# A decoder's two attentions: the low parts of the values set beside the high ones, two matmul passes in place of three, and the two halves of the output bank added afterwards

## The reference, cut to what matters

```
a0: y = layernorm(x); q, k, v = y@Wq.T, y@Wk.T, y@Wv.T   (16 heads of 32)
    x = x + softmax(causal(q k.T / sqrt(32))) v @ Wo.T
a1: y = rms_norm(layernorm(x)) * w; q, k, v = y@w_in.T   (32 query heads, 8 key groups, of 64)
    q, k = rope(q), rope(k)
    x = x + softmax(causal(q k.T / 8)) v @ w_out.T
```

## Time and profile before

| | us |
|---|---|
| runs shown (3) | 1926.97, 1926.93, 1922.9 (median 1926.93) |
| profiled execution | 1936.33 |
| its span, first to last instruction | 1934.9 |
| TensorE busy | 1813.6 (94%) |
| VectorE, ScalarE, GpSimd busy | 1116.9, 804.9, 1009.1 |
| mean granted TensorE clock | 0.980 of 2.4 GHz |

### The profile page before, as it was taken

One profiled execution on the slowest core, in us unless ns is written; L12 is line 12 of the kernel. 1 busy time (PEld: TensorE's weight loads), 2 busy tenths in 40 slices (PEclk: granted clock), 3 DMA queues, 4 the chain that ended last, 5 costly groups with the idle time before them and its releaser, 6 DMA issues.

```text
span 1934.9 us, 30810 instructions
## 1 busy us (share of the span) xinstructions
PE 1813.6 (94%) x10167; PEld 1568.5 (81%) x10167; DVE 1116.9 (58%) x2769; ACT 804.9 (42%) x2063; POOL 1009.1 (52%) x965
## 2 busy tenths in 40 slices
PE   7999989989799999999889999999999999999896
PEld 5888867778799999898668888888888888867795
DVE  6667785663233333335766666666665757566344
ACT  3766633222122222221257556665564433543231
POOL 3444342487773957895456556455453203116783
PEclk9999999999899999999999999999999999999998
DMA  3556430156553545544343243233321210012655
GB/s 116 171 154 202 138 136 35 58 182 220 179 181 132 197 161 179 188 153 118 90 115 93 66 105 103 56 89 98 80 69 55 73 50 1 24 49 98 207 199 191
DMA packets 104552, 232.54 MB, mean 120 GB/s; under 512 B 20673, under 2 KB 20929, under 8 KB 101329
## 3 DMA queue, kind: packets, MB, share of 16 engines
q1 hardware_dynamic: 84080, 144.31, 24.7%
q0 software_dynamic: 19744, 85.47, 13.4%
q10 hardware_dynamic: 576, 0.79, 0.2%
HBM read 126.23 MB, written 57.93 MB: 95 GB/s over the span
## 4 chain that ended last, share of the span: by engine, by line
PE 55%; DVE 5%; POOL 4%; issue 3%; DMA 3%; SPq 3%; ACT 2%; another core or an unknown queue 1%; POOLq 0%; DVEq 0%; ACTq 0%
PE bank L153 45%; PE bank L1025 2%; PE bank L1009 2%; PE bank L2188 2%; PE bank L2179 2%; SPq L669 1%; DMA a_g<-a_f 1%; POOL a_g L700 1%; SPq L654 1%; DMA a_QL<-a_g 1%; POOL f_UL L165 1%; POOL a_E L706 1%; DVE X L1894 1%; PE bank L2940 1%
## 5 line engine op out<-in xcount | busy, mean ns | idle before, releaser
L706 POOL TENSOR_SCALAR a_E<-a_E,a_inv 128x128 f32<-128x128 f32 (+3 forms) x384 | 222.1, 596 | 219.9 <-DVE a_inv L842 219.9
L153 PE MATMUL bank<-f_UH,f_XH 128*128 x596 | 200.8, 337 | 22.9 <-POOL f_UL L165 12.3
L739 ACT ACTIVATE a_E<-a_E,a_top 128x512 f32<-128x512 f32 (+3 forms) x384 | 211.1, 567 | 5.1 <-DVE a_top L836 5.0
L153 PE MATMUL bank<-f_UH,f_XL 128*128 x596 | 193.6, 325 | 0.0
L153 PE MATMUL bank<-f_UL,f_XH 128*128 x596 | 193.5, 325 | 0.0
L731 ACT ACTIVATE a_PHL<-bank 128x512 fp32r<-128x512 f32 (+1 forms) x288 | 131.0, 528 | 133.1 <-PE bank L1025 133.0
L153 PE MATMUL bank<-a_PHL,a_VH 128*128 128x512 f32 (+3 forms) x768 | 180.4, 324 | 0.3 <-DVE a_QL L165 0.3
L836 DVE CUSTOM_DVE_ANT_0 a_E<-a_causal,bank 128x512 f32<-128x512 bf16 (+3 forms) x384 | 163.8, 482 | 28.0 <-PE bank L1009 16.2
L1837 DVE TENSOR_TENSOR f_gate<-bank,f_gate 128x352 f32<-128x352 f32 x79 | 41.4, 525 | 206.6 <-PE bank L153 180.5
L165 DVE TENSOR_TENSOR a_PHL<-bank,a_PHL 128x512 fp32r<-128x512 f32 (+1 forms) x288 | 153.8, 588 | 10.1 <-ACT a_PHL L731 10.0
L1782 ACT ACTIVATE f_HH<-bank 128x256 fp32r<-128x256 f32 x220 | 59.9, 324 | 239.5 <-PE bank L2179 211.9
(11 more groups left out here) (407 smaller groups left out, 4954.3 us busy)
## 6 DMA issues: line engine op xcount, KB each, us to landing
f_uraw<-f_up POOLq DMA_DIRECT2D x18, 1408.0 KB
f_xb<-table SPq DMA_DIRECT2D x86, 256.0 KB
table<-f_ob SPq DMA_DIRECT2D x86, 256.0 KB
table<-a_zeros SPq DMA_DIRECT2D x31, 512.0 KB, 3.9
f_draw<-f_down POOLq DMA_DIRECT2D x27, 512.0 KB
a_g<-a_f SPq DMA_DIRECT2D x160, 64.0 KB, 2.0
a_raw<-a_qkv SPq DMA_DIRECT2D x36, 256.0 KB
f_uraw<-f_up POOLq DMA_DIRECT2D x9, 704.0 KB
```

Source lines behind the costliest of these rows:

```text
L153: m = pe.matmul(out, a, b, start=first and i == 0 and j == 0, stop=last and i == n - 1 and j == 2, skip_group_check=not check)
L706: e.tensor_scalar(self.E[sl][:, a], self.E[sl][:, a], self.inv[:, sl, i:i + 1], 0.0, ALU.mult, ALU.add).then_inc(*self.s_nrm.up(N, m - 1, i))
L739: x = e.activation(E, E, ACT.Exp, scale=-1.0, bias=self.top[:, sl, i:i + 1], accum_out=self.total[:, sl, i:i + 1])
```

## The change

The values are kept once, in V: a head's high part in its own columns, its low part in the same place of the other half of the 128 columns (for hd 64: head 0 has high in 0 to 63 and low in 64 to 127, head 1 the other way round). Two matmuls for each key block, V with PH and V with PL, give high x (PH + PL) in one half of the bank's rows and low x (PH + PL) in the other. The two halves are then added. As both halves are in use at once, the bank is opened and emptied for each half of the heads: after every second job in a0, after every job in a1. ScalarE writes the rounded own half to QH and copies the other half, shifted by 64 partitions, to S; VectorE, one loop step later than before (m-4), right behind the reciprocal, writes own half minus QH to R; when both halves of a pair are there, GpSimd adds R + S into QL, in loop step m+4 of the last job, behind the rotation's product and ahead of the normalising. The output products wait for that (`s_rest`). In a0 the transposes of the values move ahead of the output products of their slot. The memsets of VH and VL (L683) become one of V in a0 and none in a1.

```
-        self.VH, self.VL = sb("VH", ...), sb("VL", ...)
+        self.V = sb("V", [heads, NT, P], F32R)
+        self.S, self.R = sb("S", [T]), sb("R", [T])
...
-                         [("O", 4, -1), ("O", 5, -1), ("T", 1)],
+                         [("T", 1), ("O", 4, -1), ("O", 5, -1)],
...
-                         [("O", 0), ("O", 1), ("T", 0, 1)]]
+                         [("T", 0, 1), ("O", 0), ("O", 1)]]
...
+    def opens(self, h):
+        return h * self.hd % self.HALF == 0
+    def closes(self, h):
+        return (h + 1) * self.hd % self.HALF == 0
+    def low_columns(self, cs):
+        at = (cs.start + self.HALF) % P
+        return slice(at, at + self.hd)
...  (pool, between the rotation's product and the normalising)
+            if 4 <= m < self.M + 4 and self.jobs[m - 4][3] == self.heads - 1:
+                j, b, r, h = self.jobs[m - 4]
+                e.wait_ge(*self.s_olo.after(N, j, r, b, self.half(h)))
+                e.tensor_tensor(self.QL[:, r, b * T:b * T + T], self.R[:, :], self.S[:, :], ALU.add).then_inc(
+                    *self.s_rest.up(N, j, r, b))
...  (act, end of the loop step)
-            if 3 <= m < self.M + 3 and self.jobs[m - 3][3] == self.heads - 1:
+            if 3 <= m < self.M + 3 and self.closes(self.jobs[m - 3][3]):
...
                 e.wait_ge(*self.s_av.after(N, m - 3))
-                e.activation(self.QH[:, r, b * T:b * T + T], self.k.bank[self.OB][:, :], ACT.Copy).then_inc(
+                if m - 3 >= self.heads:
+                    e.wait_ge(*self.s_rest.after(N, *self.pair(m - 3 - self.heads)))
+                e.activation(self.QH[own, r, b * T:b * T + T], bank[own, :], ACT.Copy)
+                e.activation(self.S[own, :], bank[other, :], ACT.Copy).then_inc(
+                    *self.s_ohi.up(N, j, r, b, self.half(h)))
...  (dve, behind the reciprocal; the old low part at the end of the step goes)
+            if 4 <= m < self.M + 4 and self.closes(self.jobs[m - 4][3]):
+                self._dve_low_values(m - 4)
...
+        e.wait_ge(*self.s_ohi.after(*key))
+        if m >= self.heads:
+            e.wait_ge(*self.s_rest.after(N, *self.pair(m - self.heads)))
+        low_part(e, self.R[own, :], bank[own, :], self.QH[own, r, a]).then_inc(*self.s_olo.up(*key))
...  (pe, output products and values)
-                    e.wait_ge(*self.s_olo.after(N, j, self.queries[-1], g // TT))
+                    e.wait_ge(*self.s_rest.after(N, j, self.queries[-1], g // TT))
...
-        if h == 0 and self.OB in emptied:
+        if self.opens(h) and self.OB in emptied:
...
-                t = product(e, self.k.bank[self.OB][:, sblk * P:T],
-                            [(self.VH[:, h, b * TT + sblk, :], self.VL[:, h, b * TT + sblk, :])],
-                            [(self.PH[m % 2][:, a], self.PL[m % 2][:, a])],
-                            first=h == 0 and sblk == 0, last=h == self.heads - 1 and ci == 2)
+                for x, weights in enumerate((self.PH, self.PL)):
+                    t = e.matmul(self.k.bank[self.OB][:, sblk * P:T], self.V[:, h, b * TT + sblk, :], weights[m % 2][:, a],
+                                 start=self.opens(h) and sblk == 0 and x == 0, stop=self.closes(h) and ci == 2 and x == 1)
```

More of the change, by code:

```diff
@@ L452, in __init__ @@
                          [self.E[i][:, a * D:(a + 1) * D] for i in range(self.SLOTS) for a in range(2)], rms)
+        self.HALF = P // 2
         self.head_rows = [(h, slice(h * hd, h * hd + hd)) for h in range(heads)]
@@ L527, in plan @@
             sig, ("lo", "vlo", "mx", "inv", "plo", "x", "olo", "p1", "p3"))
+        self.s_rest = sig("u")
         self.s_zero, self.s_wlo, self.s_p2, self.s_nrm = map(sig, ("zero", "wlo", "p2", "nrm"))
@@ L596, in plan @@
                 self.s_av.plan((N, m))
+                if self.closes(h):
+                    for s in (self.s_ohi, self.s_olo):
+                        s.plan((N, j, r, b, self.half(h)))
                 if h == self.heads - 1:
-                    self.s_ohi.plan((N, j, r, b))
-                    self.s_olo.plan((N, j, r, b))
+                    self.s_rest.plan((N, j, r, b))
     def moves(self, j, c, b):
@@ L615, in moves, with half, pair, halves @@
                 [(self.KH[up, 1, a], g[dn, :]), (self.KH[dn, 1, a], g[dn, :]), (self.KL[dn, 1, a], f[dn, :])]]
+    def half(self, h):
+        return h * self.hd // self.HALF
+    def opens(self, h):
+        return h * self.hd % self.HALF == 0
+    def closes(self, h):
+        return (h + 1) * self.hd % self.HALF == 0
+    def pair(self, m):
+        j, b, r, h = self.jobs[m]
+        return j, r, b
+    def low_columns(self, cs):
+        at = (cs.start + self.HALF) % P
+        return slice(at, at + self.hd)
+    def halves(self, h):
+        own = slice(self.half(h) * self.HALF, (self.half(h) + 1) * self.HALF)
+        return own, slice((1 - self.half(h)) * self.HALF, (2 - self.half(h)) * self.HALF)
     def out_weights(self, x, r):
@@ L681, in pool @@
         e.memset(self.causal[:, :], 0.0).then_inc(*self.k.g.up())
-        for z in (self.VH, self.VL):
-            e.memset(z[:, :, :, :].bitcast(F32), 0.0)
+        if 2 * self.hd < P:
+            e.memset(self.V[:, :, :, :].bitcast(F32), 0.0)
         last = self.causal[:, T - P:T]
@@ L755, in act @@
                 self._act_rotated(m - 1)
-            if 3 <= m < self.M + 3 and self.jobs[m - 3][3] == self.heads - 1:
+            if 3 <= m < self.M + 3 and self.closes(self.jobs[m - 3][3]):
                 j, b, r, h = self.jobs[m - 3]
+                own, other = self.halves(h)
+                bank = self.k.bank[self.OB]
                 e.wait_ge(*self.s_av.after(N, m - 3))
-                e.activation(self.QH[:, r, b * T:b * T + T], self.k.bank[self.OB][:, :], ACT.Copy).then_inc(
-                    *self.s_ohi.up(N, j, r, b))
+                if m - 3 >= self.heads:
[3 more added lines that the diff above has]
+                    *self.s_ohi.up(N, j, r, b, self.half(h)))
     def _act_rotated(self, m):
@@ L796, in _act_fill @@
                 for h, cs in self.head_rows:
[L797 removed]
+                    i = e.activation(self.V[:, h, b * TT:b * TT + TT, cs], src[:, :, cs], ACT.Copy, scale=1.0)
                 i.then_inc(*self.s_vhi.up(N, j, b))
@@ L861, in dve, with _dve_low_values @@
                 self.norm.dve_rest(i)
-            if 3 <= m < self.M + 3 and self.jobs[m - 3][3] == self.heads - 1:
-                j, b, r, h = self.jobs[m - 3]
-                a = slice(b * T, b * T + T)
-                e.wait_ge(*self.s_ohi.after(N, j, r, b))
-                low_part(e, self.QL[:, r, a], self.k.bank[self.OB][:, :], self.QH[:, r, a]).then_inc(
-                    *self.s_olo.up(N, j, r, b))
+    def _dve_low_values(self, m):
+        e, N, (j, b, r, h) = self.k.dve, self.name, self.jobs[m]
+        (own, other), a, key = self.halves(h), slice(b * T, b * T + T), (N, j, r, b, self.half(h))
+        bank = self.k.bank[self.OB]
+        e.wait_ge(*self.s_ohi.after(*key))
+        if m >= self.heads:
+            e.wait_ge(*self.s_rest.after(N, *self.pair(m - self.heads)))
+        low_part(e, self.R[own, :], bank[own, :], self.QH[own, r, a]).then_inc(*self.s_olo.up(*key))
     def _stats(self, loaded, tiles):
@@ L1041, in _pe_values @@
                 a = slice(self.P_AT[sblk], self.P_AT[sblk] + T - sblk * P)
-                t = product(e, self.k.bank[self.OB][:, sblk * P:T],
-                            [(self.VH[:, h, b * TT + sblk, :], self.VL[:, h, b * TT + sblk, :])],
-                            [(self.PH[m % 2][:, a], self.PL[m % 2][:, a])],
-                            first=h == 0 and sblk == 0, last=h == self.heads - 1 and ci == 2)
+                for x, weights in enumerate((self.PH, self.PL)):
+                    t = e.matmul(self.k.bank[self.OB][:, sblk * P:T], self.V[:, h, b * TT + sblk, :], weights[m % 2][:, a],
+                                 start=self.opens(h) and sblk == 0 and x == 0, stop=self.closes(h) and ci == 2 and x == 1)
         t.then_inc(*self.s_av.up(N, m))
-        if h == self.heads - 1:
-            emptied[self.OB] = self.s_olo.after(N, j, r, b)
+        if self.closes(h):
+            emptied[self.OB] = self.s_olo.after(N, j, r, b, self.half(h))
     def projections_done(self):
```

3 lines of the change are left out of this document (1 added, 2 removed).

## The result

The changed kernel takes **1988.05 us** (median of 5 runs, 1983.58 to 1991.32) where the kernel before takes 1926.93 in the same comparison (5 runs): ratio 1.032, 95% interval 1.0302 to 1.0337. It is slower by 61 us where 27.6 were forecast: the sign is right, the size less than half of it, and the time lies outside the range given.

What follows compares the result with a forecast made beforehand. TensorE was taken as the bound. Terms -58.5 + 11.0 + 38.8 + 16.5 + 6.3 + 13.5 = +27.6 us on 1926.93 gave 1954.5, forecast 1954 us, range 1928 to 1970.

Steps and rivals of the forecast that it cites:

- Part 1: Values' third matmul pass removed in both attentions: 0.61 us saved a job, 58.5 us in all.
- Part 2: Second attention (a1): stalls behind the rotation chain and in slot 5 give back 0.61 us in 18 jobs, 11.0 us.
- Parts 3 and 4: Output products wait for GpSimd's sum: 38.8 us in a1 (six waits of 6.0), 16.5 us in a0 (2.35 each).
- Part 5: Emptying the bank per job: hidden inside the a1 loop, exposed at the ends of both attentions, 6.3 us in all.
- the extra copies and halves: nothing: ScalarE's +14.4 us and VectorE's +5.5 in 130 leave both under 100 of 120 us, so no cost.
- Part 6: TensorE's clock falling behind idle waits: 9.8 us for six long ones, 3.7 for a0's, 13.5 in all.
- A: Rival: a1's long waits stay short, tipping at 2.4 us of wait with its clock loss; faster, 1909 us, chance 0.11.
- C: Rival: waits come, but their cost is taken from stalls that would follow anyway, clock holds; 1925 us, chance 0.09.
- B: Rival: ScalarE falls behind and sets the pace of a1's projection slots; 21 us more, 1975 us, chance 0.10.

Runs made afterwards that it cites:

- e5: Kernel before without the third pass (values' low part times weights' high part), drain per pair, product incomplete: 1911.3 us, 0.9858 of the kernel before.
- e4: Changed kernel without the sum, values' low part left out of the output, still two passes and a drain per job: 1937.2 us, 0.9992 of the kernel before.
- e13: e5 with three slots of f and g in a1 and ScalarE evicting the new projection first: 1893.7 us, 0.9752 of the kernel before.
- e14: e4 with three slots of f and g, product incomplete: 1923.9 us, 0.9896 of the kernel before.
- e9: e4 with VectorE's half of the drain at the end of the step whose values closed it: 1919.0 us, 0.9968 of the kernel before.
- e11: Changed kernel with VectorE's half at the end of its own step and VectorE also doing the sum: 1971.1 us, 1.0245 of the kernel before.
- e1: Changed kernel plus idle matmuls on TensorE ahead of each output product that waits for the sum: 1978.3 us, 1.0192 of the kernel before.
- e2: Changed kernel with GpSimd's sum issued ahead of the rotation product instead of behind it: 1981.3 us, 1.0227 of the kernel before.
- e3: Changed kernel with VectorE doing the sum right behind its low part, instead of GpSimd: 1962.3 us, 1.0115 of the kernel before.

## Why the prediction was right in its sign and wrong in its size

**Part 1, right as work, wrong as gain with Part 2: the step that failed first.** The pass is 0.61 us a job. But I let a1 lose it in five jobs of an output step, and the chain that takes it begins one tile sooner than I began it: not at S(1), but with the tile evicted in slot 15 (and 7). I had the row for its pace, the query evicted late at 1245.49 behind moves, and took the chain from S(1) because the stall showed behind it. In e5, slots 15 to 3 in three output steps and slots 7 to 11 in four take 2.2 us less than before, all told; I had left them 12.8 (21 of 35 jobs). Besides, slots 0 and 4 of e5's a0 keep the length that they had in six of seven cases, 7.85 us in five of them: a score there waits for VectorE's additions into X (3.7 us); and e5 loses 17 us to the clock, where the two profiles of the kernel before lose 7.8 and 12.6, in part within the same slots. Forecast -47.5, shown -25 to -27: 20 us.

**Parts 3 and 4, right.** Six waits of 6.0 forecast, 36.0 us measured; with a0's and the ends' 59.1 forecast, 56.7 measured. The place (right behind the key's rotation) and the price of a0's wait (2.35 against 2.13) hold.

**Part 5 and "the extra copies and halves: nothing", wrong by 20 us.** I had VectorE's half out 3.9 us after the scores start, from slots where VectorE begins its maxima at S + 1.4. In slot 3 it begins at S + 2.9 and the half is out at S + 5.4 (1288.78 against 1283.42), after TensorE wants it. e5 to e4 shows 26 to 28 us, e13 to e14 19.5 in a1. That both engines stay under their budget on average says nothing about order: ScalarE now stops at the end of each job for TensorE's values. What share ScalarE has in it and what VectorE stays open: e9 to e11 moved VectorE's half and shifted the waits only.

**Part 6, mis-sized by some 20 us: the largest single term.** Forecast 13.5, traced 36.8 (32 against the second profile of the kernel before). I let a third of a0's waits drop the clock from one row each way (2.33 did, 1.50 did not); the waits were 2.13 to 3.44 and all eight did. The long ones cost 1.7 to 3.0 (13.4 in six), not 1.6 each, and the shorter new waits of Parts 2 and 5 have their own: 5 to 9 us in e5, some 4 more in e4. e1 shows the 25 us behind the waits for the sum directly.

**How the three add up.** They overlap: the first two are read from runs, which lose to the clock as well. Laid along the runs, the forecast is -47.5 for the pass (e5), +6.3 for the drains (e4) and +68.8 for the sum, its waits and the clock; measured are -27, +26 and +63. The last is below its forecast although the clock was priced too low, because in e4 TensorE already waits 19.4 us at the same output products.

**Rivals.** A and C didn't come: the waits were all there. A's tipping point was mis-worked, too: 18.2 us over six waits are 3.0 each with the clock loss, so it tips at 1.4 us of wait, not at 2.4. B (ScalarE behind) foresaw a price for the copies and the right direction, at 21 us; the drains' 26 us are its size, but its mark, slots at ScalarE's pace throughout, is missing: slots 15, 0, 4, 5, 7, 12 and 13 kept their 0.61. What decides is which slots stand in a chain, not an engine's load.

## What to carry to other kernels

Before a slot is credited with a saving, follow the chain of the other resource back to its first link, by the spacing of its rows (here four rotation products 8 us apart). Price a new wait on TensorE together with the clock behind it: here 57 us of waits cost 25 us more, and idle matmuls in them won those back. Twice as many drains are an edit of their own, and cost as much as the removed pass brought.

## What was not expected of the hardware

Idle stretches of barely 2 us can halve TensorE's clock, and their length alone does not decide it. The clock fell to 0.50 behind all six stretches of 2.13 us in the changed kernel's a0. In e2 it fell behind five of six such stretches and stayed at 1.00 behind the first:

```profile
78.36 0.47 PE L153 MATMUL bank<-a_WH,a_QH 128*128 128x512 f32 x1 [2.13 <-POOL a_QL L727]
```

```profile
78.00:80.00 2.00, 1.65 (x7) 1.42 (x8) 0.99 (x5) 1.49 (x8) 2.00 (x5) 1.00 0.39 98
```

In e3's a0 it stayed at 1.00 behind six of 1.52 us, and for the 3 us of matmuls behind one of 2.83 (before 244.02). At the end of e5's a0 it fell behind one of 1.50 us; the same stretch in the kernel before (before 240.31) had left it at 1.00:

```profile
229.72 0.77 PE L153 MATMUL bank<-a_WH,a_QH 128*128 128x512 f32 x1 [1.50 <-DVE a_QL L165]
```

```profile
230.00:232.00 2.00, 2.00 (x6) 1.52 (x6) 0.63 (x1) 0.00 (x0) 0.00 (x0) 0.50 0.00 0
```

A fall in a0 costs 1.6 to 1.7 us of TensorE's time even if the wait is barely over 2 us.

GpSimd's rotation product takes 1.76 to 1.80 us where VectorE's product (0.69) began 0.05 us ahead of it, 32 times in the kernel before, and 1.29 to 1.33 where it began first itself, five times, with VectorE's then stretched to 1.78 to 1.80, as in the earlier trace rows; so 1.79 us, which the prediction takes as its usual time, holds a wait. VectorE's addition of the rotation takes 778 ns on average before and 1271 after, because GpSimd's sum stands beside about half of them:

```profile
L884 DVE TENSOR_TENSOR a_f<-a_f,a_g 128x512 f32<-128x512 f32 x38 | 29.6, 778 | 40.2 <-POOL a_g L700 40.0
```

```profile
L930 DVE TENSOR_TENSOR a_f<-a_f,a_g 128x512 f32<-128x512 f32 x40 | 50.8, 1271 | 47.4 <-POOL a_g L729 47.3
```
